# Attention tiles worked on as two halves of 64 tokens, and reciprocals spread as two 16-bit parts

## What is computed

```
x = x + windowed_attention(layernorm(x))     # |query - key| <= 128 tokens, scale 1/16, output projection Wp
x = x + mixture_of_experts(layernorm(x))     # 8 experts, top 2, and a shared one
x = x + block_attention(layernorm(x))        # blocks of 64 tokens: first and last block see all 1024 keys,
                                             # each other block sees blocks 0 and last, itself and its neighbours
x = x + ternary_linear(x)                    # (input normalised too)
```

## Time and profile before

| | |
|---|---|
| three runs | 2443.06 us median (2439.72 to 2443.52) |
| the profiled execution's own time | 2437.45 us |
| its span | 2435.7 us |
| PE, DVE, ACT, POOL busy, share of the span | 90%, 76%, 68%, 44% |
| TensorE clock granted, mean | 0.947 of full |
| instructions on PE | 25,549 matmuls, as many weight loads |

### The profile page before, as it was taken

The page is one execution under the profiler, slowest core; times in us unless marked ns, Lnnn a source line. Parts: engine busy times, 40 slices in busy tenths (PEclk is TensorE's granted clock), DMA queues, the critical chain, the costliest instruction groups (busy, mean ns, idle before and its releaser), DMA issues. The chain is left out here.

```text
span 2435.7 us, 73430 instructions
## 1 busy us (share of the span) xinstructions
PE 2200.0 (90%) x25549; PEld 1344.8 (55%) x25549; DVE 1840.5 (76%) x5599; ACT 1661.7 (68%) x3892; POOL 1072.9 (44%) x1370
## 2 busy tenths in 40 slices
PE   7979999999969688879999995996999999999765
PEld 4643444444436576768888884563444444444354
DVE  5539999999829577755445444984999999999298
ACT  7955888889942555525445443893699999999644
POOL 3533666666654466646666664562000000000076
PEclk9987999999979899989999998997899999999888
DMA  6552333333232567646654344884232232322242
GB/s 231 199 183 72 91 91 92 92 90 92 67 89 77 138 189 187 163 129 125 144 127 106 92 92 118 270 274 149 63 80 74 78 79 78 79 75 68 65 152 96
DMA packets 363698, 289.65 MB, mean 119 GB/s; under 512 B 228401, under 2 KB 296753, under 8 KB 363345
## 3 DMA queue, kind: packets, MB, share of 16 engines
q1 hardware_dynamic: 349616, 248.24, 37.2%
q0 software_dynamic: 12960, 35.60, 4.5%
q10 hardware_dynamic: 768, 1.12, 0.2%
HBM read 133.53 MB, written 123.69 MB: 106 GB/s over the span
## 5 line engine op out<-in xcount | busy, mean ns | idle before, releaser
L740 ACT ACTIVATE a_pr<-a_pst 128x384 f32<-128x384 f32 (+3 forms) x2176 | 908.8, 486 | 117.0 <-PE a_pst L775 79.7
L775 PE MATMUL a_psc<-a_ke,a_qe 52*128 52x128 f16 (+5 forms) x3072 | 648.6, 291 | 32.7 <-DMA a_ke<-mrow 29.2
L692 DVE TENSOR_REDUCE a_mx<-a_psc 128x1 f32<-128x384 f32 (+2 forms) x1152 | 566.9, 564 | 18.9 <-PE a_psc L775 13.7
L775 PE MATMUL a_pst<-a_qe,a_ke 53*128 53x128 f16 (+5 forms) x3072 | 564.3, 281 | 2.7 <-ACT a_pr L740 0.4
L836 PE MATMUL a_po<-a_pr,a_ve 128*17 128x128 f32 (+3 forms) x10496 | 562.1, 302 | 2.0 <-ACT a_pr L740 1.2
L687 DVE CUSTOM_DVE_ANT_0 a_cut<-a_psc,row_mask 128x384 bf16<-128x384 f32 (+1 forms) x1024 | 472.7, 521 | 23.4 <-PE a_psc L775 11.5
L775 PEld LDWEIGHTS a_pst<-a_qe,a_ke 53*128 53x128 f16 (+1 forms) x3072 | 210.3, 94 | 330.1 <-ACT a_pr L740 187.5
L658 POOL TENSOR_SCALAR_AFFINE_SELECT a_pr<-a_pr 128x512 f32<-128x512 f32 x448 | 275.1, 634 | 163.2 <-ACT a_pr L740 163.2
L775 PEld LDWEIGHTS a_psc<-a_ke,a_qe 52*128 52x128 f16 (+1 forms) x3072 | 223.5, 94 | 143.7 <-DVE a_mx L692 44.5
L836 PEld LDWEIGHTS a_po<-a_pr,a_ve 128*17 128x17 f32 x10496 | 193.9, 96 | 191.2 <-issue 116.3
L638 POOL TENSOR_SCALAR a_mneg<-a_mx 128x32 f16<-128x32 f32 x64 | 18.4, 288 | 632.5 <-DVE a_mx L696 588.1
(11 more groups left out here) (234 smaller groups left out, 4172.7 us busy)
## 6 DMA issues: line engine op xcount, KB each, us to landing
a_qe<-qx SPq DMA_DIRECT2D x378, 64.0 KB, 2.6
a_ke<-kx SPq DMA_DIRECT2D x378, 64.0 KB, 2.7
vx<-p_vst SPq DMA_DIRECT2D x32, 544.0 KB, 3.4
a_ve<-vx SPq DMA_DIRECT2D x64, 272.0 KB, 3.1
qx<-p_stg SPq DMA_DIRECT2D x64, 256.0 KB, 3.4
kx<-p_stg SPq DMA_DIRECT2D x64, 256.0 KB, 3.3
ox<-a_ost SPq DMA_DIRECT2D x256, 64.0 KB
x_res<-x SPq DMA_DIRECT2D x16, 512.0 KB, 8.9
```

The costliest lines, as they stand in the source:

```text
L692: dve.tensor_reduce(out.unsqueeze(1), psc[(u * n_s + n) % RING][:, 0:width], AXX, ALU.max)\
L740: act.activation(pr[s % SLOTS][:, h // 2, h % 2, 0:width], pst[prob_slot(u, n) % RING][:, 0:width], ACT.Exp, scale=scale).then_inc(p_ready, 1)
L775: last = pe.matmul(out[:, col:col + count], stat, mov(tok, count), start=(k == 0), stop=(k == len(pieces) - 1), skip_group_check=True, til ...
```

## The change

1. **Half tiles.** `product` now splits each score and probability tile into two halves of 64 keys in different column halves of TensorE. Both halves do the 256 columns that they share (two matmuls), then each its own 64 columns (`edges`, two more, into the same 64 columns of the bank). A tile that was 384 wide becomes 320. In a0 the probability tile gets two more matmuls, which add the mask of the edge columns (`corner16`). The 256 and 512 wide tiles become two matmuls of the full width.
2. **Values.** The 64 edge columns hold other queries for keys 0 to 63 than for 64 to 127, so `with_v` does them twice, with `vez`: values with one half of the keys zeroed. `vez` is loaded by 2 more DMAs per unit (`load_v`), and zeroed once on GpSimd. The value product of a 384 job is cut into pieces of 128, 64, 128, 64 columns, split into equal parts by `v_split`; before, 192 and 192, or 256 and 128. For the 512 wide jobs it is 4 pieces of 128 where it was 2 of 256.
3. **Masks and constants.** a0 loads a mask table (`corner`, 128 x 512) on ScalarE's queue; GpSimd's cuts shrink from 4 x 128 to 4 x 64 columns in the inner jobs. a1's `brows` are gone.
4. **Combine.** The reciprocals are split into two 16-bit parts, on ScalarE (`high`) and VectorE (`low`), twice in the stage; the spreading product is two 16-bit matmuls where it was one in 32 bits.

```diff
--- before.py
+++ after.py
-    jobs = []
-    for t in range(TB):
-        lo, hi = max(0, t - 1), min(TB, t + 2)
-        masks = []
-        if t > 0:
-            masks.append((0, P, 0))
-        if t < TB - 1:
-            masks.append(((hi - lo - 1) * P, P, 1))
-        jobs.append((t, [(lo * P, (hi - lo) * P, 0)], masks))
-    return jobs
+    jobs = [(0, [(0, 2 * P, 0)], None, [(P, P, 1, 0)])]
+    for t in range(1, TB - 1):
+        lo = t * P - 64
+        jobs.append((t, [(lo, 2 * P, 0)], (lo - 64, lo + 2 * P, True, True), [(0, 64, 0, 64), (3 * 64, 64, 1, 0)]))
+    return jobs + [(TB - 1, [(N - 2 * P, 2 * P, 0)], None, [(0, P, 0, 0)])]
...
-    jobs = [(0, [(512, 512, 0)], [])]
+    jobs = [(0, [(512, 512, 0)], None, [])]
     for t in reversed(range(1, TB)):
-        lo, hi = max(P, t * P - 64), min(N, t * P + P + 64)
-        jobs.append((t, [(0, P, 0), (lo, hi - lo, P)], []))
-    return jobs + [(0, [(0, 512, 0)], [])]
+        left, right = t > 1, t < TB - 1
+        edges = (t * P - 64 if left else t * P, t * P + P if right else t * P + 64, left, right)
+        jobs.append((t, [(0, P, 0), (t * P, P, P)], edges, []))
+    return jobs + [(0, [(0, 512, 0)], None, [])]
...
-    KS = TK + (0 if const_rows is None else 4)
+    KS = TK
...
+        vez = sb("vez", [P, 2, HG, TB, 4 * VW], F32)
+        EM = 2 * P + 64
+        if masked:
+            cut, corner, corner16 = sb("cut", [P, 4, EM], BF16), sb("corner", [P, EM + 192], F32), sb("corner16", [P, 192], BF16)
...
-        def v_cuts(s):
-            out = []
+        def v_pieces(s):
+            shared, edges = [], []
             for tok, count, col in jobs[s][1]:
                 while count:
-                    w = min(count, CH - tok % CH)
-                    out.append((tok, w, col))
+                    w = min(count, CH - tok % CH, P if count > 3 * 64 else count)
+                    shared.append((0, tok, w, col))
                     tok, count, col = tok + w, count - w, col + w
+            if jobs[s][2]:
+                a, b, left, right = jobs[s][2]
+                edges = [(1, a, 64, widths[s] - 64)] * left + [(2, b, 64, widths[s] - 64)] * right
+            out = []
+            for n in range(max(len(shared), len(edges))):
+                out += shared[n:n + 1] + edges[n:n + 1]
+        def v_split(s):
+            ws = [p[2] for p in v_pieces(s)]
+            return min(range(1, len(ws)), key=lambda n: abs(sum(ws[:n]) - sum(ws[n:])))
...
-                sp.dma_start(ve[g][:, :, :], vx[bass.ds(b * N, N), g * 4 * VW:(g + 1) * 4 * VW]
-                             .rearrange("(t p) w -> p t w", p=P)).then_inc(v_loaded[g], 16)
+                v = vx[bass.ds(b * N, N), g * 4 * VW:(g + 1) * 4 * VW].rearrange("(t p) w -> p t w", p=P)
+                sp.dma_start(ve[g][:, :, :], v).then_inc(v_loaded[g], 16)
+                for half in range(2):
+                    r = slice(64 * half, 64 * half + 64)
+                    sp.dma_start(vez[r, half, g, :, :], v[r, :, :]).then_inc(v_loaded[g], 16)
...
+                pool.memset(vez[64:P, 0, :, :, :], 0.0).then_inc(vez_set, 1)
+                pool.memset(vez[0:64, 1, :, :, :], 0.0).then_inc(vez_set, 1)
+                pool.wait_ge(vez_set, 2)
...
-                    for col, width, which in jobs[s][2]:
+                    for col, width, which, base in jobs[s][3]:
                         edge = pr[s % SLOTS][:, :, :, col:col + width].rearrange("p i a c -> p (i a) c")
                         sign = 1 if which == 0 else -1
-                        pool.affine_select(out=edge, in_=edge, compare_op=ALU.is_ge, fill=0.0, base=0,
+                        pool.affine_select(out=edge, in_=edge, compare_op=ALU.is_ge, fill=0.0, base=base,
...
-                        at = 0 if t > 0 else P
+                        mask = corner[:, 0:width] if edges else row_mask[:, 0:width] if t else row_mask[:, P:P + width]
...
+                if masked:
+                    act.dma_start(corner[:, :], edge_masks).then_inc(c_loaded, 16)
                 for g in range(HG):
                     for par in range(2):
-                        r = slice(par * 64 + TK, par * 64 + KS)
-                        if const_rows is not None:
-                            act.dma_start(qe[g][r, :, :], const_rows[0]).then_inc(rows_set[g], 16)
-                            act.dma_start(ke[g][r, :, :], const_rows[1]).then_inc(rows_set[g], 16)
                         act.dma_start(ke[g][par * 64 + KS:par * 64 + KR, :, :], mrow[:, :].unsqueeze(1).to_broadcast([1, 2, N])).then_inc(rows_set[g], 16)
...
-            def product(par, out, stat, mov, pieces, ready):
-                for k, (tok, count, col) in enumerate(pieces):
-                    last = pe.matmul(out[:, col:col + count], stat, mov(tok, count), start=(k == 0),
-                                     stop=(k == len(pieces) - 1), skip_group_check=True, tile_position=(64 * par, 0))
+            def product(par, out, t, stat, mov, job, cornered, ready):
+                _t, pieces, edges, _m = job
+                end = sum(p[1] for p in pieces)
+                halves = [slice(64 * half, 64 * half + 64) for half in range(2)]
+                for half in range(2):
+                    if len(pieces) == 2:
+                        to = out[halves[half], 0:end].rearrange("p (t c) -> p t c", c=P)
+                        of = mov.rearrange("k (t c) -> k t c", c=P)[:, 0:t + 1:t, :]
+                    else:
+                        to, of = out[halves[half], 0:end], mov[:, pieces[0][0]:pieces[0][0] + end]
+                    last = pe.matmul(to, stat[:, t * P + 64 * half:t * P + 64 * half + 64], of, start=True, stop=True,
+                                     skip_group_check=True, tile_position=(64 * par, 64 * half))
+                for half in range(2) if edges else ():
+                    last = pe.matmul(out[halves[half], end:end + 64], stat[:, t * P + 64 * half:t * P + 64 * half + 64],
+                              mov[:, edges[half]:edges[half] + 64], start=False, stop=True, skip_group_check=True,
+                              tile_position=(64 * par, 64 * half))
+                for half in range(2) if edges and cornered else ():
+                    r = slice(64 * par, 64 * par + 64)
+                    last = pe.matmul(out[halves[half], end:end + 64], corner16[r, 0:64], corner16[r, 64 + 64 * half:128 + 64 * half],
+                              start=False, stop=True, skip_group_check=True, tile_position=(64 * par, 64 * half))
                 last.then_inc(ready, 1)
...
+                opened = {h for q in range(s) for h in range(2) if touches(q, h)}
+                for n, (kind, tok, w, col) in enumerate(v_pieces(s)):
                     h = tok // CH
-                    if (n < middle) == (part == 0):
+                    if (n < v_split(s)) == (part == 0):
                         for a in range(4):
+                            cols = slice(a * VW, (a + 1) * VW)
+                            stat = vez[:, kind - 1, g, t, cols] if kind else ve[g][:, t, cols]
                             last = pe.matmul(po[h][32 * a:32 * a + VW, tok % CH:tok % CH + w],
-                                             ve[g][:, t, a * VW:(a + 1) * VW], pr[s % SLOTS][:, a // 2, a % 2, col:col + w],
+                                             stat, pr[s % SLOTS][:, a // 2, a % 2, col:col + w],
...
-        self.spread = ctx.enter_context(nc.sbuf_tensor(f"{tag}_spread", [P, B * EC * P], F32))
+        self.rec_hi = ctx.enter_context(nc.sbuf_tensor(f"{tag}_rec_hi", [P, N], F16))
+        self.rec_lo = ctx.enter_context(nc.sbuf_tensor(f"{tag}_rec_lo", [P, N], F16))
+        self.spread = ctx.enter_context(nc.sbuf_tensor(f"{tag}_spread", [P, B * EC * P], F16))
...
+    def high(self, act, half):
+        cols = slice(half * CH, half * CH + CH)
+        act.wait_ge(self.ready, half + 1)
+        act.activation(self.rec_hi[:, cols], self.rec[:, cols], ACT.Copy, scale=SHS).then_inc(self.high_done, 1)
+    def low(self, dve, half):
+        cols = slice(half * CH, half * CH + CH)
+        dve.wait_ge(self.high_done, half + 1)
+        dve.scalar_tensor_tensor(out=self.rec_lo[:, cols], in0=self.rec[:, cols], scalar=SHS, in1=self.rec_hi[:, cols],
+                                 op0=ALU.mult, op1=ALU.subtract).then_inc(self.low_done, 1)
     def over_rows(self, pe, out, c, e):
         if c < 2:
             pe.wait_ge(self.set, 3)
-            pe.wait_ge(self.ready, c + 1)
+            pe.wait_ge(self.low_done, c + 1)
         at = ((c // 2) * EC + e) * P
-        return pe.matmul(out, self.spread[:, at:at + P], self.rec[:, (c % 2) * CH:(c % 2) * CH + CH],
-                         start=True, stop=True)
+        cols = slice((c % 2) * CH, (c % 2) * CH + CH)
+        pe.matmul(out, self.spread[:, at:at + P], self.rec_hi[:, cols], start=True, stop=False)
+        return pe.matmul(out, self.spread[:, at:at + P], self.rec_lo[:, cols], start=False, stop=True)
```

88 lines of the change are left out of this document (49 added, 39 removed).

## The result

The changed kernel takes **2534.6 us** (median of 4 runs, 2525.0 to 2538.1) where the kernel before takes 2442.9: ratio 1.037, 95% interval 1.034 to 1.040. The forecast was 2442, range 2404 to 2480. The profiled execution took 2535.78 us, 98.3 more than that of before. Window attention a0 is 68.3 us longer (165.3 to 761.6 us), block attention a1 33.4 (1738.6 to 2399.0), all the rest together 3 shorter.

What follows compares the result with a forecast made beforehand. It took TensorE to bound a1 and SyncE's queue a0. a0 +37.6, combine -6.8 and a1 -30 gave +0.8 on the profiled 2437.45 us, so 2438.2; allowing for that profile's luck, 2442 us, range 2404 to 2480.

Steps and rivals of the forecast that it cites:

- VectorE's saving: Half tiles in a1: each 384 tile saves VectorE 0.066 us, its pace becomes 0.40 us, its job 1.6 us.
- TensorE's half job in a1: In a1, two pairs of tiles at 0.41 us plus the value product at 0.455 us, a job of 1.73 us.
- the new bound: In a1, TensorE instead of VectorE becomes the bound, with units of 17.25 us where they were 18.04.
- Rival D: Half tiles' weight loads don't hide, 0.055 us each; a1's units stay at 18.0 us, 2466 us in all; chance 0.08.
- Rival B: Every matmul has a floor of 24 ns; a1's job becomes 1.89 us, 2476 us in all; chance 0.11.
- the fetch term: More instruction fetches cost SyncE's queue 0.57 us each: +1.4 us per unit in a0, +1.1 in a1.
- Rival C: TensorE's issue is the limit at 58 ns per matmul, +810 us, about 3250 us in all; chance 0.03.
- a1: -30 forecast: Block attention's sum: start -2.3, score tiles alone -2.6, 30 units x -0.8 = -24, the end -1.3 us.
- a0: +37.6 forecast: Window attention's sum, mostly 27 intervals lengthened from 15.24 to 16.9 us by SyncE's queue, +45 us.
- the sign that it bounds: In a0, TensorE's idle time at each unit's start ended by a DMA into `a_qe` would show SyncE's queue bounding.
- The term for two pairs in a0: In a0, two pairs of tiles take 0.42 us, bounds 0.40 to 0.50, the mask adding one short pair per probability tile.
- Combine: -6.8 forecast: 16-bit spreading in combine: 14 chunks x 0.4 us, limited by VectorE's idle time, = -5.6, and -1.2 at the start.

Runs made afterwards that it cites:

- e4_novez: The changed kernel with the two `vez` loads only in the first four units of each stage, leaving out part of the output: 2516.7 us.
- e7_vpool: The changed kernel with `vez` made on GpSimd out of `ve` in place of the two loads per unit: 2516.5 us.
- e10_fewer: e7_vpool with 816 TensorE instructions per a0 unit for 1008, by joined columns and larger value pieces, same products and columns: 2470.3 us.
- e16_slowmax: e7_vpool with a1's maxima taken in a0's form (addition of a mask, here zeros, then a read of the accumulator): 2521.7 us, one run.
- e1_combine: The kernel before with only the combine part of the change (reciprocals spread as 16-bit halves), both attentions as before: 2434.5 us, ratio 0.9973.
- e11_gpmask: e10_fewer with the mask of a0's edge columns as one GpSimd multiplication per job, for two matmuls per probability tile: 2464.7 us.
- e14_mix3: The kernel before with 16-bit spreading, `vez` made on GpSimd, and half tiles in only 3 of a1's 5 jobs of 384: 2420.5 us.
- e15_mix5: e14_mix3 with all 5 of a1's jobs of 384 as half tiles, the other jobs still full tiles: 2434.4 us.

## Why the prediction was wrong

- **VectorE's saving, TensorE's half job in a1, the new bound: right.** Two pairs took 0.41 (0.41 forecast), a half job 0.87 (0.865), the unit without stalls 17.41 (17.25). Rival D falls with it. Rival B falls too: 64 column value passes took 56 ns per four (and its 16 x 0.024 + 0.09 is 0.47, not 0.49, which would have made the job no longer than now).
- **The step that failed is the fetch term: it charges SyncE's queue alone, and puts TensorE's own wait for its program at nothing, without a reason.** On the queue it was right: 82 of 106 fetches in 235 to 690 us stand beside an issue that took over 0.9 us, 0.60 us too long per fetch (0.57 forecast), and with 10.6 us of waits in 400 the queue works 17.1 us per unit (16.9 forecast). But a fetch also costs TensorE, for which it carries the program: the gaps at block boundaries are 1.7 us per unit in a1 and 1.8 in a0, and that was in neither the sum nor a rival. Rival C had the right resource, TensorE's instruction supply, but took its limit from the densest stretch of before, 58 ns per matmul, which VectorE had paced; the blocks with a wait took 4.33 us per 256 instructions, 17 ns each, or some 34 ns per matmul with its load. C's 810 us are eight times the 98 measured, and it got 3 in 100. The trace of before has no row for it: in both its attentions 256 TensorE instructions never went by in under 5.6 us. So what happens at the forecast 17.25 / 4.5 = 3.8 us was unknown. I had bounded operations from both sides, but not this rate.
- **a1: -30 forecast, +33.4 measured.** The unit is 2.0 us over its undisturbed 17.41, 1.7 of it in gaps at block boundaries; over 30 units that is 60 us. The rest is the 17.41 for 17.25.
- **a0: +37.6 forecast, +68.3 measured, and the reason given is mostly not the true one.** The queue did get fuller, and its waits went near zero, as forecast. But the sign that it bounds, TensorE idle at each unit's start until a DMA into `a_qe`, stood only 4 times in 21.6 units, and two issues less per unit gave 0.4 to 0.5 us of 2.3 (e4_novez, e7_vpool), removing instructions 1.4 (e10_fewer). Two limits lay close to each other: 17.1 us for the queue, and 17.1 for TensorE with its stalls once the queue had room (e7_vpool). That the forecast had the right sign in a0 is in good part luck. The term for two pairs in a0 was mis-sized too: 0.42 (to 0.50) forecast, 0.45 to 0.54 measured, with VectorE's masked form as the likely cause (e16_slowmax). a0 could not have gained: its half jobs' medians are 15.3 for 15.18.
- **Combine: -6.8 forecast, -7.2 measured** (e1_combine). The chunk became 0.52 us shorter for 0.42, and VectorE paces it, as forecast. a1's start: the first matmul waited 13.74 us for 15.69 of the earlier trace rows, -2.0 for -2.3.

The TensorE waits are told first by the rows above. The Trainium skill, "Runtime: NRT & Kernel Launch", section "Instruction fetch mechanics", says that the sequencer fetches blocks of 16 KB, 256 instructions, while it executes the current one, and that this is hidden since instructions issue more slowly than they are filled in. The trace agrees on the size of a block, 256 instructions, and disagrees on the hiding: 44 of 87 blocks of a1 ended in a wait. I did not weigh this page of the Trainium skill; its rule, taken with the 1056 instructions per unit, would have made me ask how fast a fill is.

What stays open: why a fetch starts 1.8 us after a boundary, and what fills the 1.4 us between the end of its transfer and TensorE's next instruction. The wait for the program is inferred from the counts, the queue and the experiments; no row of the profile names it. That the low clock in short stretches of the changed kernel (0.93 in 400 to 500 us) comes from the stalls is likely, since each stretch follows one and e10_fewer has 1.00 there, but wasn't tried by itself. Where e11_gpmask's remaining 15.26 us lie wasn't settled.

## What to carry to other kernels

Before an edit that trades columns for more and smaller matmuls, work out how long 256 of TensorE's instructions (matmuls, weight loads and semaphore waits) will take where they are densest: here blocks of under 3.7 us mostly ended in a wait when they followed each other (51 of 65 in a1), blocks of over 4.2 us hardly ever (2 of 40), whatever the engines' busy shares said. Stalls that end in "issue", at fixed counts of the engine's instructions, point to the program's own fetch. Spread the dense stretches out among sparse ones, as e14_mix3 did, before looking for fewer instructions; and before believing that a full queue bounds, relieve it in one run.

## What the hardware showed that I had not expected

- TensorE's program arrives in blocks of 256 instructions, and blocks that end in a wait take about the same in all kernels here: medians of 4.33 us in the changed kernel's a1, 4.18 in its a0, 4.23 with 50 GB/s of traffic in place of 87, 4.20 with full tiles, 4.28 in e15_mix5. It isn't a hard limit: after a slow block a fast one (3.3 to 3.6 us) can pass free of a wait, and six blocks in a row went by at a mean of 3.9 us.
- A probability or score tile made of one matmul of 128 and two of 64 stationary columns took 2.8 times as long as one of halves alone (1.49 us for two pairs at the full clock, 0.54 in the changed kernel's a0), and the kernel's mean granted clock was 0.67 where it had been 0.94.
- An addition of a mask with a maximum, followed by a read of the accumulator (83 ns), made the next tile start 0.10 to 0.15 us later, although VectorE's own instruction is no longer (489 ns for 320 columns, 483 for the plain maximum of the earlier trace rows). That the score bank comes free later is how I read it; no row shows it.
